# Gate products in four column groups, a second value tile ahead of the last projection, and x2's transposes in four transfers

## The reference, cut to what matters

```python
x = x + mlstm(layernorm(x))          # 8 heads, 32 query/key and 64 value features each
x = x + ffn(layernorm(x))            # 512 -> 2048 -> 512, weights -1/0/+1, gelu

# inside mlstm, h = layernorm(x):
q, k, v, o = h @ Wq.T, h @ Wk.T, h @ Wv.T, h @ Wog.T
i_pre = 15 * tanh((h @ Wig.T + big) / 15)      # input gate, 8 rows (heads) x 512 tokens
f_pre = 15 * tanh((h @ Wfg.T + bfg) / 15)      # forget gate, 8 rows x 512 tokens
# per token: f_log = log_sigmoid(f_t); m_new = max(f_log + m, i_t)
#            C = exp(f_log + m - m_new) * C + exp(i_t - m_new) * outer(k, v); n likewise
#            head = (q C) / (max(|q n|, exp(-m_new)) + eps)
y = (sigmoid(o) * multihead_norm(head)) @ Wout.T
```

## Time and profile before

| | us |
|---|---|
| median of three runs | 1786.42 |
| profiled execution, its own time | 1786.99 |
| its span, first to last instruction | 1785.3 |
| TensorE busy (matmul) | 1739.6 |
| VectorE busy | 1425.1 |
| ScalarE busy | 1069.4 |
| GpSimd busy | 605.8 |

### The profile page before, as it was taken

How to read it: one execution, slowest core, us unless ns; L and a number is a source line. 1 busy time by engine, 2 the same in 40 slices (tenths; PEclk the granted TensorE clock), 3 DMA queues, 4 the chain that set the end, 5 groups by cost and what they waited for, 6 DMA issues and landing times.

```text
span 1785.3 us, 31702 instructions
## 1 busy us (share of the span) xinstructions
PE 1739.6 (97%) x12192; PEld 867.9 (49%) x12192; DVE 1425.1 (80%) x2526; ACT 1069.4 (60%) x1801; POOL 605.8 (34%) x481
## 2 busy tenths in 40 slices
PE   5779999999999999999999999999999999999999
PEld 3464444444454444444444454444444444444555
DVE  6787978788797878978887897878879787886872
ACT  5877648375673837557373754737466483746743
POOL 1241432524234252432425143252414325242340
PEclk8899999999999999999999999999999999999999
DMA  8433335262433626243262524426243352424120
GB/s 290 163 107 103 83 98 125 54 149 56 119 86 74 149 56 151 56 122 85 55 163 62 133 63 119 100 54 156 58 127 79 98 122 54 127 57 122 33 54 24
DMA packets 255846, 177.76 MB, mean 100 GB/s; under 512 B 200128, under 2 KB 221632, under 8 KB 250576
## 3 DMA queue, kind: packets, MB, share of 16 engines
q1 hardware_dynamic: 254112, 172.59, 37.4%
q10 hardware_dynamic: 1584, 3.15, 0.5%
HBM read 96.47 MB, written 20.23 MB: 65 GB/s over the span
## 4 chain that ended last, share of the span: by engine, by line
PE 89%; DVE 4%; ACT 2%; issue 1%; POOL 1%; DMA 0%; POOLq 0%; DVEq 0%; SPq 0%; ACTq 0%
PE pf L2032 23%; PE pf L2048 22%; PE pa L1885 20%; PE pa L1861 9%; PE psh L1885 7%; PE psh L1988 2%; PE psh L1943 1%; PE pa L1852 1%; PE psh L2022 1%; PE psh L1924 1%; PE pa L1988 1%; PE psh L1899 1%; PE psh L1984 1%; DVE den L1493 0%; DVE kT L1520 0%
## 5 line engine op out<-in xcount | busy, mean ns | idle before, releaser
L2048 PE MATMUL pf<-w2T,gT 128*128 128x512 f16 x2048 | 505.8, 379 | 0.0
L2032 PE MATMUL pf<-x2T,w1T 128*128 128x512 f16 x1920 | 422.0, 379 | 0.0
L2032 PEld LDWEIGHTS pf<-x2T,w1T 128*128 128x128 f16 x1920 | 185.5, 98 | 222.5
L2048 PEld LDWEIGHTS pf<-w2T,gT 128*128 128x128 f16 x2048 | 195.5, 97 | 177.1
L1574 DVE SCALAR_TENSOR_TENSOR gT<-g,wscale,gT 128x512 f16<-128x512 f32 x240 | 212.0, 883 | 59.7 <-ACT gT L996 57.8
L1885 PE MATMUL pa<-wT,xT 128*128 128x512 f16 x960 | 213.7, 380 | 1.0 <-ACT sig L919 0.9
L993 ACT ACTIVATE g<-pf,b1c 128x512 f32<-128x512 f32 x240 | 164.1, 684 | 75.6 <-PE pf L2032 63.6
L996 ACT ACTIVATE gT<-g,wscale 128x512 f16<-128x512 f32 x240 | 173.2, 722 | 7.9
L1885 PE MATMUL pa<-wT,shared 128*128 128x512 f16 x768 | 176.2, 379 | 1.6 <-DMA shared<-qT 1.6
L1001 ACT ACTIVATE ktok<-kT 128x512 f32<-128x512 f32 x64 | 40.3, 630 | 222.2 <-DVE kT L1498 222.2
L1861 PE MATMUL pa<-xT,wT 128*128 128x512 f16 x768 | 171.3, 379 | 0.1
(11 more groups left out here) (242 smaller groups left out, 2781.5 us busy)
## 6 DMA issues: line engine op xcount, KB each, us to landing
dec<-gate_r SPq DMA_DIRECT2D x32, 1024.0 KB, 6.1
xin<-L_attn_x SPq DMA_DIRECT2D x16, 1024.0 KB, 6.2
out<-x1b SPq DMA_DIRECT2D x64, 256.0 KB, 2.2
xres<-L_attn_x SPq DMA_DIRECT2D x16, 512.0 KB, 6.2
xres<-L_attn_x SPq DMA_DIRECT2D x32, 256.0 KB, 4.3
qw<-gate_w SPq DMA_DIRECT2D x128, 48.0 KB, 5.8
s<-state_w SPq DMA_DIRECT2D x60, 97.5 KB, 2.3
qw<-kT SPq DMA_DIRECT2D x120, 48.0 KB, 2.0
```

What stands on the lines that cost most here:

```text
L2032: last = nc.tensor.matmul(bank, w1T[:, k, tok(f)], x2T[:, part, :, k, :], start=(k == 0 and part == HI), stop=(k == KD - 1 and part == LO))
L2048: last = nc.tensor.matmul(bank, gT[:, part, f, tok(t)], w2T[:, f, :], start=(f == 0 and part == HI), stop=(f == NF - 1 and part == LO), sk ...
```

## The change: what it does

1. `gates` puts the four feature groups into four column groups of 32 columns, at PSUM partitions 0, 32, 64 and 96. The 12 matmuls stay 12, in another order, and four partial sums come out in place of two. ACT copies the one at 96, and DVE adds three, one after the other, before the bank is free. The gate rows are now eight forget rows and, right behind them, eight input rows.
2. Input gate rows lie in partitions 8 to 15 of `th`, and the scans need them in 0 to 7. SP moves them with a small transfer into `gi` as soon as tanh is done; DVE waits for it (`i_loaded`) at the head of `gate_decay` and scales `gi` there.
3. The value products of tile 1 stand ahead of projection 3, no longer behind it.
4. The gate columns stand behind the first query product, on TensorE and on ACT.
5. SP: the two loads of `dec` stand ahead of the store of `gate_w`; x2 is transposed in four transfers (two halves of the tokens, high and low), each half as soon as its parts are there; the xres load follows; the eight `qw` loads come last.
6. The copy of qw's columns to `fcol` on DVE stands behind the first two feed-forward tiles, and on POOL `layer_norm(b + 1)` stands ahead of `weigh_queries`.

```diff
-    GATE_F = 32
-    GROWS = GATE_F + NH
+    GROWS = 2 * NH
+    QUAD = P // KD
...
             def gate_rows(b):
+                sp.wait_ge(tanh_ok, at(b, 1, 1))
+                sp.dma_start(gi, th[NH:GROWS, :]).then_inc(i_loaded, 16)
                 sp.wait_ge(r_ok, at(b, 1, 1))
                 sp.dma_start(gate_r[b], th[0:NH, :]).then_inc(r_stored, 16)
-                sp.wait_ge(gate_act, at(b, 5, 4))
-                sp.dma_start(gate_w[b], ge[:, 0:LATE]).then_inc(w_stored, 16)
...
+                sp.wait_ge(gate_act, at(b, 5, 4))
+                sp.dma_start(gate_w[b], ge[:, 0:LATE]).then_inc(w_stored, 16)
+
+            def query_rows(b):
...
             def transpose_x2(fb):
+                for n, half in enumerate(HALVES):
+                    sp.wait_ge(part2_ok, at(fb, 2, n + 1))
+                    for part in (HI, LO):
+                        sp.dma_start(x2T[:, part, half, :, :].rearrange("p t k c -> p (t k) c"),
+                                     parts2[:, part, half, :].rearrange("p t d -> p (t d)"),
+                                     transpose=True).then_inc(x2T_loaded, 16)
                 residual(fb + 1, RES_TILES[0])
-                sp.dma_start(x2T[:, :, :, :, :].rearrange("p a t k c -> p (a t k) c"),
-                             parts2.rearrange("p a t d -> p (a t d)"), transpose=True).then_inc(x2T_loaded, 16)
...
                 gate_rows(b)
                 transpose_x2(b - 1)
+                query_rows(b)
                 transpose_x(b + 1)
...
-                nc.scalar.activation(th, pa[P // 2:P // 2 + GROWS, pa_bank(b, U_GATE), :], ACT.Copy).then_inc(gate_lo, 1)
+                nc.scalar.activation(th, pa[3 * QUAD:3 * QUAD + GROWS, pa_bank(b, U_GATE), :], ACT.Copy).then_inc(gate_lo, 1)
...
                     keys(b, 1)
+                    queries(b, 0)
                     gate_columns(b)
-                    queries(b, 0, 1)
+                    queries(b, 1)
...
             def gate_sum(b):
+                bank = pa_bank(b, U_GATE)
                 dve.wait_ge(gate_lo, at(b, 1, 1))
-                nc.vector.tensor_tensor(th, pa[0:GROWS, pa_bank(b, U_GATE), :], th,
-                                        ALU.add).then_inc(pa_free[pa_bank(b, U_GATE)], 1)
+                nc.vector.tensor_tensor(th, pa[2 * QUAD:2 * QUAD + GROWS, bank, :], th, ALU.add).then_inc(gate_part, 1)
+                dve.wait_ge(gate_part, at(b, 2, 1))
+                nc.vector.tensor_tensor(th, pa[QUAD:QUAD + GROWS, bank, :], th, ALU.add).then_inc(gate_part, 1)
+                dve.wait_ge(gate_part, at(b, 2, 2))
+                nc.vector.tensor_tensor(th, pa[0:GROWS, bank, :], th, ALU.add).then_inc(pa_free[bank], 1)
...
-                nc.vector.tensor_scalar(gi, th[0:NH, :], CAP, None, ALU.mult)
-                nc.vector.tensor_scalar(gf, th[GATE_F:GROWS, :], CAP, 0.0, ALU.mult, ALU.min)
+                nc.vector.tensor_scalar(gf, th[0:NH, :], CAP, 0.0, ALU.mult, ALU.min)
...
+                dve.wait_ge(i_loaded, at(b, 16, 16))
+                nc.vector.tensor_scalar(gi, gi, CAP, None, ALU.mult)
                 dve.wait_ge(gate_arg, at(b, 3, 3))
...
             def gates(b):
                 bank = take_pa(b, U_GATE)
-                for k in range(KD // 2):
-                    for n, (ws, xs) in enumerate(PARTS):
-                        for half, rows_of in enumerate((slice(0, P // 2), slice(P // 2, P))):
-                            kc = 2 * k + half
-                            last = nc.tensor.matmul(bank[rows_of, :], wgT[:, kc, ws, :], xT[:, xs, :, kc, :],
-                                                    start=(k == 0 and n == 0), stop=(k == KD // 2 - 1 and n == 2))
+                for n, (ws, xs) in enumerate(PARTS):
+                    for k in range(KD):
+                        last = nc.tensor.matmul(bank[k * QUAD:(k + 1) * QUAD, :], wgT[:, k, ws, :], xT[:, xs, :, k, :],
+                                                start=(n == 0), stop=(n == 2), skip_group_check=True)
                 last.then_inc(pa_fill, 1)
...
                     x_ready(b + 1)
                     gates(b + 1)
                     tokens(b + 1, U_V, xT[:, :, 0, :, :], C_V)
+                    late_values(b + 1, 1)
                 project(b, 3)
```

More of the change, by code:

```diff
@@ L130, in block_program @@
         wT = sb("wT", [P, 2, KD, 4 * D], F16)
-        wgT = sb("wgT", [P, KD, 2, P // 2], F16)
+        wgT = sb("wgT", [P, KD, 2, QUAD], F16)
         w1T = sb("w1T", [P, KD, FF], F16)
@@ L266, in block_program @@
         gate_lo, tanh_ok = sem("gate_lo"), sem("tanh_ok")
+        gate_part, i_loaded = sem("gate_part"), sem("i_loaded")
         gate_arg = sem("gate_arg")
@@ L466, in _ @@
                     sp.wait_ge(s_const, 1)
[L467 to L470, removed]
+                    sp.dma_start(th[0:NH, :], Wfg).then_inc(s_wload[4], 16)
+                    sp.dma_start(th[NH:GROWS, :], Wig).then_inc(s_wload[4], 16)
+                    sp.dma_start(gate_bias[0:NH, :], bfg.unsqueeze(1)).then_inc(s_bias, 16)
+                    sp.dma_start(gate_bias[NH:GROWS, :], big.unsqueeze(1)).then_inc(s_bias, 16)
             sp.dma_start(gcol[:, :], gamma.rearrange("h v -> (h v)").rearrange("(k p) -> p k", p=P),
@@ L576, in _ @@
             gate_rows(0)
+            query_rows(0)
             for n in range(4):
@@ L596, in _ @@
             transpose_x2(B - 2)
+            query_rows(B - 1)
             residual(B - 1, RES_TILES[1])
@@ L715, in sequence @@
                     ternary_low()
+                elif b + 1 < B:
+                    layer_norm(b + 1)
                 weigh_queries(b)
-                if not first and b + 1 < B:
-                    layer_norm(b + 1)
                 for n in range(NH // 2):
@@ L1037, in sequence @@
                     replace_rows(G_O)
-                    gate_columns(b)
                     absolute_sums1(1)
                     queries(b, 0)
+                    gate_columns(b)
                     absolute_sums1(2)
@@ L1327, in gate_minus @@
                     dve.wait_ge(hoT_loaded[T - 1], at(b, 16, 0))
-                nc.vector.tensor_scalar(ge, th[GATE_F:GROWS, :], CAP, None, ALU.mult).then_inc(gate_arg, 1)
+                nc.vector.tensor_scalar(ge, th[0:NH, :], CAP, None, ALU.mult).then_inc(gate_arg, 1)
                 dve.wait_ge(gate_arg, at(b, 3, 1))
@@ L1601, in sequence @@
                 keys_last(b)
-                chunk_decay(b)
                 if not run_f:
+                    chunk_decay(b)
                     norm_apply(b + 1, range(T))
@@ L2029, in up @@
                     if f == 0 and k == 0:
-                        pe.wait_ge(x2T_loaded, at(fb, 16, 16))
+                        pe.wait_ge(x2T_loaded, at(fb, 64, 64))
                     for part in (HI, LO):
@@ L2095, in sequence @@
                             pe.wait_ge(s_bound, 2)
-                        late_values(b, t)
+                        if first or t > 1:
+                            late_values(b, t)
                     if first and t == 0:
@@ L2106, in sequence @@
                     prepare(USES_O[n + 2])
-                gate_columns(b)
                 for n in range(HG):
                     features(b, U_Q + n, C_QK + n * P)
+                    if n == 0:
+                        gate_columns(b)
                 if first:
```

## The result

The changed kernel takes 1805.09 us (median of 4 runs, 1803.38 to 1807.55), the kernel before 1786.51 (4 runs, 1786.16 to 1787.1). The ratio is 1.0102, with a 95% interval of 1.009 to 1.0114: 18.6 us slower, where 7 us faster were forecast. The profiled execution took 1807.55 us with a span of 1805.8, 20.5 us more than the span before.

A forecast was written before the change was run, and what follows sets the result against it. TensorE, busy throughout the steady passes, was taken as the bound. 15 x (-0.65 gate products + 0.15 store wait) + 0.6 for pass 0 = -6.9 us, giving 1779.5 us; likeliest 1776.5 to 1782.8, 8 in 10 within 1775.8 to 1787.5.

The forecast's parts named there:

- The store of `gate_w`: Store behind both `dec` loads lands at 582.45; TensorE waits 0.1 us before the output gate, 0.15 per pass taken.
- one bound only: Upper bound of the store's wait: 2 us, where the second `dec` load lands as late as 8.9 us after issue.
- its fast end: Fast end of the likeliest range, 1776.5 to 1782.8 us, if the store waits only for eight engines' share of the loads.
- The gate products: Four column groups on TensorE cut the 12 matmuls from 1.42 to 0.77 us, saving 0.65 us in 15 passes.
- rival D: Column groups overlap only in pairs, 1787 us, or not at all, 1804 us; chance 0.08.
- Queries: First query product needs the bank of the first keys, copied by ACT; TensorE waits 0 to 0.1 us.
- Projection 3 moves back: Behind tiles 0 and 1 it costs TensorE no wait; without the tile ahead it would wait 0.35 us.
- x2's transposes and `qw`: Four transposes land by 591.1 us, `qw` by 594, before their readers; costs and gives nothing.
- Pass 0: TensorE waits there for VectorE, whose list gets two new sums; +0.6 us taken, bounds 0 to +1.5.
- B: Rival: `gate_w`'s store lands 0.4 to 0.9 us later and the wait eats the saving; near 1786 us, chance 0.24.
- C: Rival: same wait, slower; 1788.8 us if five passes are held back 2 us, 1808 if all; chance 0.09.

The follow-up runs named there:

- store_on_act: The changed kernel, but ScalarE issues the store of `gate_w` on its own queue, right behind the exp that makes it; 1789.59 us, ratio 1.0017.
- tile1_first: The changed kernel with the `gate_w` store ahead of the `dec` loads again and value tile 1 ahead of tile 0; 1780.83 us, ratio 0.9967 to the kernel before.
- keys_first: tile1_first, and ScalarE copies the first keys ahead of the high parts of x2's first half; 1777.84 us, ratio 0.9951 to the kernel before.
- no_tile_ahead: keys_first with value tile 1 behind projection 3 again, only tile 0 ahead of it; 1787.19 us, ratio 1.0001 to the kernel before.
- four_transfers_only: The kernel before with one edit, x2's transposes in four transfers at their old place; 1786.7 us, ratio 0.9999.

## Why the prediction was wrong

**The step that failed is "The store of `gate_w`".** Its mechanism was right, and named as what decides; its size was not. I had the store land 7.3 us after the first load's issue and TensorE wait 0.1 us, 0.15 as the mean of a pass. Measured, that term is 1.34 us per pass, 1.19 of recorded wait and 0.15 of lost overlap, and 3.4 us in all at half clock beside it. In the pass shown it landed near 591.22, 591.22 - 583.17 = 8.05 us after that issue. The difference to the 0.79 us that TensorE waited is worked out from the same rows: landing +0.75; `gate_r` leaves 0.18 later than I had it (its path grew from 14.77 to 15.95 us behind the gates, 1.18, not 1.0, since tile 0's stop delays projection 3 too); `dec` follows it after 1.52 us, not 1.4, +0.12; TensorE itself is late by the two small waits, -0.22 - 0.18. That gives 0.1 + 0.75 + 0.18 + 0.12 - 0.40 = 0.75, against 0.79. The largest single error is the 0.75. The forecast stood on two arrivals that came out 0.1 us apart at the end of some 25 us, with only 0.65 us per pass to be gained, and each microsecond that the store is late costs 15.

**What 7.3 stood on.** It was the latest landing of `qw`, another transfer behind the same loads. But the row that belongs to the question is the landing of the later load itself, since the store came in right behind it: 7.5 us in the pass shown now, 7.0 in that of before. With 7.0 for the load, 0.4 for its issue behind the first and 0.2 for the store, even the rows of before would have given 7.6, and the earlier trace rows 9.5 in the late passes. I had those rows and used them for one bound only, with the guess that a late load need not hold up eight small rows. That guess had a ground in the kernel before: in the pass of the earlier trace rows the first `qw` load, issued at 367.0, landed within 6.5 us, by 373.5, and the later `dec` load only at 375.3. Line 508 (`qw`), 360 to 384 us, issue to landing of its eight:
```profile
DMA to landing us min/median/max: 4.7/6.0/6.5
```
The store, on the same queue, did not get past. In the three passes with waits of 2.5 to 2.6 us it took 7.6 to 7.7 us and landed behind the load. The count of late passes was off too: the loads that took 8.9 us or more stand in four passes of the kernel before, not five, and two more took 8.1.

The Trainium skill ("DMA: Bandwidth & Descriptors", section "Why a DMA increments its semaphore by 16 and not by 1") has such a transfer on eight of the engines only; that each engine takes its ring in order stands in that page's section "Queues, rings and completion order". I held that this would bring the sum nearer to its fast end. On SP's queue it did not, in any of the 15 passes. On ScalarE's queue the store did land ahead of the later load (store_on_act). No run here tells the engines apart, so why it does on one queue and not on the other stays open.

**The gate products**: right. 0.77 us forecast, 0.76 in the chain; rival D fell with it. The rows that were to show four groups side by side proved less than I made of them: 119 to 17 ns is seven to one, more than four groups can give, so something beside the overlap is in it. The Trainium skill's figure for three groups ("TensorE: Matmul & The Clock Gate", section "Why this matters for your kernels") gave an estimate of 3.2 times for four; measured, 2.59 / 0.76 is 3.4.

**Missing: tile 0's bank.** The prediction let tile 0 follow the gates at once. Its bank is freed by the residual of projection 2 (L1550), which before had the longer gate group as cover. 0.22 us per pass, 3.1 in all, shown by tile1_first.

**Queries**: "a wait of 0 to 0.1 us" was 0.18, and no matmul has a wait on record there; it shows in the weight load's line (7.4 us, 15 times) and in the group's 8.11 us. 2.7 us in all, shown by keys_first.

**Projection 3 moves back**: right. It doesn't wait, and without the tile ahead it would lose 0.37 us per pass (no_tile_ahead), where I had 0.35. `gi` is there in time in steady passes, as predicted (issued 572.58, read at 577.39 without a wait).

**x2's transposes and `qw`**: right, nothing (four_transfers_only).

**Pass 0**: +0.6 forecast with bounds of 0 to +1.5, measured +1.57, just outside them. One part that I had not looked for is the small transfer of `gi`, which here stands behind loads that keep the queue full:
```profile
34.26 0.77 SPq L495 DMA_DIRECT2D sig<-qT  x1
```
```profile
40.12 0.41 DVE L1371 TENSOR_SCALAR sig<-sig 8x512 f32<-8x512 f32 x1 [0.92 <-DMA sig<-qT]
```

**The rivals.** What happened is the mechanism of B and C: the store late, from the point where TensorE is no longer held up by anything else, and each pass losing. In the pass shown the store is 1.05 us later than reckoned (0.75 + 0.18 + 0.12), just past B's 0.4 to 0.9. C had its two prices for 5 or 15 passes that are late by 2 us, 1788.8 and 1808; in fact all passes are late, 12 by 0.4 to 1.5 us and three by 2.5 or 2.6, so that the time came out near the second price for another reason. B and C together had 0.33. That was too little: with the load's own landing, 7.6 for 7.3, the forecast is already 15 x (-0.65 + 0.45) + 0.6 = -2.4 us, in B.

## What to carry to other kernels

Where a change makes the bounding engine faster and the path of another one longer, compare the two arrivals, not the sum saved: if they come out level, the forecast is a toss-up, and each further delay costs once per pass. A small transfer that something waits for goes ahead of large loads; price it behind them by the landing of the last large load, at its latest in any pass, and not by another small transfer. A queue of its own got it past a late load in two passes of three, but it still took 5.1 us. And look at which banks the shortened piece of work gave cover to: here two waits of 0.2 us per pass, of which one has no line of its own among TensorE's waits, were worth 6.2 us (1784.03 to 1777.84).

## What the runs showed of the hardware

- A stop of TensorE costs more than its wait on record: 0.22 us for 0.15, 0.94 for 0.79 (592.03 here against the 582.40 - 571.13 = 11.27 us of keys_first, with 592.03 - 579.64 = 12.39 now, less the query products' 0.18). The difference, 0.07 and 0.15, is at most the overlap of two groups that follow each other without a stop (2.75 us long, 2.60 from start to start).
- After waits of 2.59 and 2.61 us the granted clock was at about half (0.50 to 0.69 in slices of 2 us) for some 3 to 4 us and cost 1.69 us (12.22 instead of 10.53); after a wait of 2.53 us in the last pass and all shorter ones it stayed at 1.00, 10.53 us. In store_on_act a wait of 2.39 us was followed by 12.22 us too, so the length of the wait alone doesn't tell.
- 12 KB issued 2.2 us after the first of two 1 MB loads took 5.1 us on another engine's queue and 5.9 on the same queue; with no other transfer of SP's ahead 1.4. In the three passes of each run in which the later load was late (8.6 to 9.5 us), they took 7.6 to 7.7 us on the same queue, and 5.0, 5.0 and 7.6 on the other.
- The landing of the same pair of 1 MB loads varies from pass to pass of one execution: the later one took 7.5 us at 583 and 9.3 at 368.
